# A ring of 32 message slots, with gathers written out, in a graph network kernel

## The reference

```python
xn = layernorm(x)
# graph part: one MLP for messages and nodes
mlp = lambda h: relu(h @ w1 + b1) @ w2 + b2
agg = segment_sum(mlp(xn[dst]), src, N)        # 50000 gathered rows, summed by src
gnn = mlp(xn + agg)
# mix part: 8 heads of 32, second-order linear attention over all nodes
q, k, v = split(xn @ Wqkv.T + bqkv)
y = 0.5*(qn x qn):(kn x kn x v) + c1*qn:(kn x v) + c2*sum(v)   # per head, divided by its first column
x = x + gnn + y @ Wproj.T + bproj
# FFN part: 16 experts, the top 2 of each node, 256 -> 512 -> 256
x = x + layernorm(xn2 + sum_k weight_k * expert_k(xn2)) * gamma + beta,  xn2 = layernorm(x)
```

## Time and profile before

| | us |
|---|---|
| median of 3 runs | 1543.14 (1540.83 to 1543.5) |
| the profiled execution | 1546.45 |
| its span, first to last instruction | 1544.5 |
| TensorE matmuls busy | 1125.4 (73%) |
| VectorE busy | 947.2 (61%) |
| GpSimd busy | 955.1 (62%) |
| ScalarE busy | 476.4 (31%) |
| mean granted TensorE clock | 0.855 of full |
| DMA, mean over the span | 94 GB/s |

### The profile page before, as it was taken

The page is one execution under the profiler, slowest core; times in us unless marked ns, Lnnn a source line. Parts: engine busy times, 40 slices in busy tenths (PEclk is TensorE's granted clock), DMA queues, the critical chain, the costliest instruction groups (busy, mean ns, idle before and its releaser), DMA issues.

```text
span 1544.5 us, 26303 instructions
## 1 busy us (share of the span) xinstructions
PE 1125.4 (73%) x7084; PEld 769.8 (50%) x7085; DVE 947.2 (61%) x2221; ACT 476.4 (31%) x1280; POOL 955.1 (62%) x1069
## 2 busy tenths in 40 slices
PE   2978878888846677667686767776884499999900
PEld 2656534333323444334453444444784499999800
DVE  4998989999955545445454555545356534433366
ACT  1555325555502223223222222221332032322302
POOL 4598339999976666666766667666000367755416
PEclk8999988999977878688877888878996699999955
DMA  5001000000034443444444455455462222222293
GB/s 154 26 26 34 21 21 1 0 0 0 0 102 119 130 131 117 128 132 122 129 124 129 127 153 156 128 155 123 128 219 93 81 69 70 73 70 70 61 236 100
DMA packets 57119, 145.11 MB, mean 94 GB/s; under 512 B 11117, under 2 KB 24909, under 8 KB 56944
## 3 DMA queue, kind: packets, MB, share of 16 engines
q0 software_dynamic: 33488, 101.80, 22.7%
q1 hardware_dynamic: 23584, 42.74, 9.4%
HBM read 124.91 MB, written 19.59 MB: 94 GB/s over the span
## 4 chain that ended last, share of the span: by engine, by line
PE 39%; DVE 18%; another core or an unknown queue 11%; POOL 11%; issue 10%; DMA 3%; DVEq 3%; ACT 2%; SPq 1%; POOLq 0%; ACTq 0%
PE bank L1805 8%; PE bank L2057 8%; PE bank L2068 7%; POOL big L698 6%; DVE node_buf L1269 3%; DVE big L1196 3%; POOL big L641 2%; DVE big L1195 2%; PE bank L1971 2%; PE bank L1858 2%; PE bank L1866 2%; DVEq L1269 2%; DMA x_buf<-x 1%; DMA big<-xn_rows 1%
## 5 line engine op out<-in xcount | busy, mean ns | idle before, releaser
L719 POOL DMA_INDIRECT big<-msg_rows,big x416 | 422.9, 1017 | 212.7 <-issue 102.0
L1269 DVE TENSOR_TENSOR node_buf<-node_buf,bank 125x256 f32 x416 | 174.6, 420 | 301.0 <-remote 131.1
L1805 PE MATMUL bank<-big 128*128 128x256 bf16 x1248 | 218.7, 324 | 63.1 <-DVE node_buf L1269 43.2
L1805 PEld LDWEIGHTS bank<-big 128*128 128x128 bf16 x1248 | 131.8, 114 | 141.3 <-DVE node_buf L1269 65.9
L1196 DVE TENSOR_SCALAR big<-bank,big 125x416 bf16<-125x416 f16 x400 | 184.6, 480 | 0.8 <-PE bank L1678 0.8
L954 ACT ACTIVATE big<-bank 128x500 f32<-128x500 f32 (+1 forms) x208 | 109.2, 572 | 222.8 <-remote 121.9
L698 POOL TENSOR_TENSOR big<-big 125x512 f32<-125x512 f32 x150 | 170.4, 1173 | 5.1 <-PE bank L1750 2.5
L1048 ACT ACTIVATE mid<-bank,const 128x128 f32<-128x128 f32 x256 | 73.0, 368 | 208.7 <-PE bank L2057 193.0
L1678 PE MATMUL bank<-big 125*128 125x416 bf16 x400 | 105.8, 350 | 29.9 <-DVE big L1196 19.6
L2068 PE MATMUL bank<-big,mid 128*128 x512 | 121.0, 380 | 0.0
L759 POOL DMA_INDIRECT moe_rows<-mid,const x64 | 71.7, 1120 | 78.7 <-DVE mid L1585 75.0
(11 more groups left out here) (307 smaller groups left out, 2119.2 us busy)
## 6 DMA issues: line engine op xcount, KB each, us to landing
big<-L_ffn_w SPq DMA_DIRECT2D x32, 512.0 KB
big<-msg_rows,big POOLq DMA_INDIRECT x416
big<-moe_rows SPq DMA_DIRECT2D x10, 560.0 KB
msg_rows<-big SPq DMA_DIRECT2D x25, 187.5 KB
xn_rows<-mid POOLq DMA_DIRECT2D x5, 625.0 KB, 5.8
x_buf<-x SPq DMA_DIRECT2D x5, 560.0 KB
big<-xn_rows SPq DMA_DIRECT2D x5, 560.0 KB
out<-big SPq DMA_DIRECT2D x5, 560.0 KB
```

The costliest lines, as they stand in the source:

```text
L719: pool.indirect_dma_start(msgs[k], None, msg_rows, bass.IndirectOffsetOnAxis(idx_ring[:, half, k:k + 1], 0)).then_inc(msgs_in[k], 16)
L1269: dve.tensor_tensor(rows, rows, agg_ps[2 * half + j][0:P, :], ALU.add).then_inc(s.agg_add, 1)
L1805: last = mm(agg_ps[k % 4], hot_src[:, turn, k, :], msgs[slot][:, D * i:D * i + D], start=i == 0, stop=i == 2, skip_group_check=True)
```

## The change

- The ring has 32 slots: the 25 node tiles' key and value columns, three at the end of `big`, and four in `mid`, two in the place of biases and two in that of the matrices `sel_f` and `selT`, which the key part's last transposes still use. Slots 2i and 2i + 1 share a semaphore; TensorE waits for 32 more on it before both messages.
- GpSimd's gathers are written out, 416 of them, with the index column read from `edge_idx` where it lies: no copy, no loop, no increment. Gather 16 waits for the last transposes of the key part (`kvT_mm`), gather n from 32 on for message n - 32 to be consumed.
- SP loads no expert during the message stage. All 16 are loaded after the last add, expert e after 3e // 2 additions of the second pass.

```diff
-        msgs = [big[:, 3 * D * k + D:3 * D * k + D + 3 * D // 2].bitcast(BF16) for k in range(2 * GB)]
+        slot_at = [big[:, 3 * D * k + D:3 * D * k + D + 3 * D // 2] for k in range(T)]
+        slot_at += [big[:, NX * 2048 - 3 * D // 2 * (k + 1):NX * 2048 - 3 * D // 2 * k] for k in range(3)]
+        slot_at += [mid[:, at_:at_ + 3 * D // 2] for at_ in (12 * D, 12 * D + 3 * D // 2, 4 * D, 4 * D + 3 * D // 2)]
+        msgs = [view.bitcast(BF16) for view in slot_at]
...
-            early = range(-(-2 * GB * 3 * D // 2048), phase // 2048)
-            for e in early:
-                sp.wait_ge(s.split_ok, (2048 * (e + 1) - 1) // (3 * D) + 1)
-                load_expert(e)
             sp.wait_ge(s.x_ok, CHUNKS)
             sp.dma_start(b1_rows, ffn_b1.rearrange("e (c p) -> (e c) p", p=128)).then_inc(s.b1_in, 16)
 
             sp.wait_ge(s.agg_add, NBATCH * GB)
-            for i, e in enumerate([e for e in range(NX) if e not in early]):
-                if i:
-                    sp.wait_ge(s.x2_add, 2 * i)
+            for e in range(NX):
+                if e:
+                    sp.wait_ge(s.x2_add, 3 * e // 2)
                 load_expert(e)
...
-            def gather(n, half):
-
-
-                pool.tensor_copy(idx_ring[:, half, :], edge_idx[:, bass.ds(n * 2 * GB, 2 * GB)]).then_inc(s.msg_idx_ok, 1)
-                pool.wait_ge(s.msg_idx_ok, n + 1)
-                for k in range(2 * GB):
-                    if not at(n, (0,)):
-                        pool.wait_ge(s.agg_mm, n * 2 * GB + k - (2 * GB - 1))
-                        apart(pool)
-                    pool.indirect_dma_start(msgs[k], None, msg_rows,
-                                            bass.IndirectOffsetOnAxis(idx_ring[:, half, k:k + 1], 0)).then_inc(msgs_in[k], 16)
-
-            gather(0, 0)
-            gather(1, 1)
-            with pool.Fori(1, NBATCH // 4) as i:
-                gather(i * 2, 0)
-                gather(i * 2 + 1, 1)
+            for n in range(NQ):
+                if n == 2 * GB:
+                    pool.wait_ge(s.kvT_mm, 4)
+                if n >= 4 * GB:
+                    pool.wait_ge(s.agg_mm, n - (4 * GB - 1))
+                slot = n % (4 * GB)
+                pool.indirect_dma_start(msgs[slot], None, msg_rows,
+                                        bass.IndirectOffsetOnAxis(edge_idx[:, n:n + 1], 0)).then_inc(msgs_in[slot // 2], 16)
...
-            def agg_pair(n, turn, q, rounds):
+            def agg_pair(n, turn, q, half, rounds):
...
+                first = (half * 2 + turn) * GB + 2 * q
+                pe.wait_ge(msgs_in[first // 2], rounds * 32)
                 for k in (2 * q, 2 * q + 1):
-                    slot = turn * GB + k
-                    pe.wait_ge(msgs_in[slot], rounds * 16)
+                    slot = first + k % 2
...
-                        agg_pair(half * 2 + 2 + k // 4, k // 4, k % 4, half + 2)
+                        agg_pair(half * 2 + 2 + k // 4, k // 4, k % 4, 1 - g, u + 1 + g)
```

More of the change, by code:

```diff
@@ L139, in __init__ @@
         self.sorted_ok = sem("sorted_ok")
-        self.msg_idx_ok = sem("msg_idx_ok")
         self.hot_src_ok = sem("hot_src_ok")
@@ L423, in program @@
         den_ones = b.take([CH], BF16, parts=1)
-        idx_ring = b.take([2, 2 * GB], I32)
         bucket_pack = b.take([NQ // 4], parts=1)
@@ L445, in program @@
         mixT = b.take([2, CH])
+        assert b.at + 9 * D // 2 <= NX * 2048
         kvT = big[:, features:features + 1024].rearrange("p (a n) -> p a n", a=2)
@@ L1925, in _ @@
             for q in range(4):
-                agg_pair(0, 0, q, 1)
+                agg_pair(0, 0, q, 0, 1)
             q_parts_T(0, 0, 2)
-            agg_pair(1, 1, 0, 1)
-            agg_pair(1, 1, 1, 1)
+            agg_pair(1, 1, 0, 0, 1)
+            agg_pair(1, 1, 1, 0, 1)
             gram_of(0, 0, 2)
-            agg_pair(1, 1, 2, 1)
+            agg_pair(1, 1, 2, 0, 1)
             den_of(0, 0, 2)
-            agg_pair(1, 1, 3, 1)
+            agg_pair(1, 1, 3, 0, 1)
             sel_of(0, 0, 0, 2)
```

## The result

The changed kernel takes 1532.81 us (median of 4 runs, 1531.99 to 1533.02); the kernel before, run beside it, takes 1543.27 us (1540.83 to 1543.5). The ratio is 0.9936, with a 95% interval of 0.992 to 0.9953: 10.5 us or 0.6% faster. The forecast was 1541.3 us, a gain of 1.8; the time lies inside the stated range, but the gain is almost six times the forecast one.

What follows compares the result with a forecast made beforehand. TensorE's message matmuls, losing up to 0.447 us per message while gathers are in flight, were taken to bound the message stage. 1543.14 less 1.8 (end -7.2, start +5.4, all else 0) gave 1541.3 us; range 1505 to 1557.

Steps and rivals of the forecast that it cites:

- "0 us; without that cover it would be -20.5" (copy, loop, increment): GpSimd's gathers: removing 0.79 us per turn of 16 gains 0, hidden behind 106 us of waiting for TensorE; otherwise -20.5.
- the large gain: Message stage: held results delay the next gather and twice the depth breaks this loop; 1532, 1500 or 1437 us; chance 0.14.
- the even part stays as it is: Message stage once the ring is full: each gather waits for one message consumed whatever the depth, 24.8 us per 16 messages.
- Tail, -7.2 us: End of the message stage: 32 messages instead of 16 remain after the last gather, saving 16 x 0.447 = 7.2 us.
- Filling, +5.4 us: Start of the message stage: 12 of 16 extra gathers fly beside TensorE's work, costing 12 x 0.447 = 5.4 us.
- The burst rival: Start of the message stage: a 20 us longer gather burst delays TensorE; +2, stronger case 1556, up to 1569; chance 0.26.
- The net of the ends, -1.8: Start and end of the message stage with 32 slots: -7.2 and +5.4 us together give -1.8 us.
- Pair semaphore, 0: TensorE's waits for messages: one semaphore for two slots removes 208 waits, priced at 0 us; 42.6 us at most.
- Expert loads, 0: Message stage: the three expert weight loads moved out of it aren't felt there, 0 us.
- Second pass, 0: After the last add: 20 MB move instead of 17, DMA doesn't set the pace; 0 us, up to 6 at the routing.
- The floor of 1.25 us for a gather: GpSimd in the message stage: a gather takes 0.95 us plus 0.30 of gap, also when written out.
- The signs: What traces would show: right, 24.8 us per 16 messages and GpSimd waits 100 or more; wrong, shrinking or filling over 10 longer.

Runs made afterwards that it cites:

- set one: Four kernels on one chip, kernel before 1474.35 us: 16 slots 0.9764, same with early expert loads 0.9772, only gathers written out 0.9872, only pair semaphore 0.9951.
- set three: One chip, kernel before 1552.87 us: 16 slots 0.9836, kernel before written out with copies 0.9872, 16 slots with third of bytes 0.9845, SyncE's loads instead of gathers 0.8517.
- set two: One chip, kernel before 1473.87 us: kernel before unedited 1.0002, the change 0.9762, 16 slots 0.9767, 32 slots opened slowly 0.9755.

## Why the prediction was right or wrong

- **"0 us; without that cover it would be -20.5" (copy, loop, increment): the step that failed.** Alone it gave 21.1 us in set one, where GpSimd sets the pace, and with only the copies kept 19.1 in set three, where GpSimd waits for held results; by the timelines the part taken away there is 15.9 us of GpSimd's time. The cover, 106 us of GpSimd's waiting for TensorE, wasn't one. Nor did it "only grow": it fell to 89.5. Of the step's 0.79 us per turn the copy is only 0.18, and the turn ahead of the loop shows that most of the rest isn't the loop. The rival of the large gain described such a loop, in which GpSimd's waiting is part of what delays it; it had 0.14. What shows is that GpSimd's own work lies on the path even there. By which route isn't settled. The end of the filling, where a result comes through as GpSimd has to stop, would fit a lock-step of the two: held results stop GpSimd, its stop lets them through, and GpSimd's own work and TensorE's waiting then add up instead of overlapping. No run tests this by itself.
- **"the even part stays as it is": wrong, by 21.1 us.** It measured 47.8 us for 32 messages after 49.8. Of the depth itself the step was nearly right: with 16 slots 16.6 of the 21.1 stay, and in set two depth changes nothing (0.9762 and 0.9767).
- **Tail, -7.2 us: right mechanism, half its size.** It measured -14.6. TensorE's idle time in the last 32 messages fell from 41.30 - 28.99 = 12.3 to 3.0 us, which is 9.3; the other 5.3 are busy time, 28.99 to 23.66, at a clock that rose from 0.83 to 1.00. The sum had priced idle time alone.
- **Filling, +5.4 us: wrong size, +22.7.** The reason given, "TensorE waits for another chain there", failed: the transposes of that chain ran 11 us earlier, and TensorE still stood for 25.07 us. The burst rival had this right. Its stronger case was 20 us lost, 7.2 won back, and with 16 slots in set three the filling is 65.9, as before.
- **The net of the ends, -1.8:** +22.7 - 14.6 = +8.1 by the windows. By these, 32 slots alone would have been a loss on this chip, less whatever of the even part's 21.1 is theirs (4.5 by the window with 16 slots).
- **Pair semaphore, 0: wrong where GpSimd sets the pace,** 7.0 us (4.3 to 10.2 by the interval); the 42.6 us of "issue" that I set aside as held results bounded it. Where results are held it wasn't tried alone.
- **Expert loads, 0: right.** 1439.10 and 1438.06 us. **Second pass, 0: right.** Outside the message stage the spans have 890.2 and 888.7 us (1.0 of the difference is the earlier first gather), and the distance at the routing stayed 6.9.
- **The floor of 1.25 us for a gather: right.** From one gather to the next it is 1.24 us at least and 1.25 in the median, in all 13 traces with gathers.
- **The signs.** Of those for being wrong, two came at once: the even part shrank (23.9 us per 16 messages where 24.8 were to stay), the sign of the large gain, and the filling grew by over 10 us, that of the burst. GpSimd's waits fell below the 100 us that the forecast wanted. Three pieces of 15 to 23 us made a net of 13, of which the forecast had 1.8. That the time fell inside the range was luck as much as anything: two rivals, one up and one down, came true together and cancelled for the most part.

## What to carry to other kernels

Waiting time on an engine is cover only if the engine isn't part of the loop that it waits on: here 106 us of waiting hid next to nothing of 20.5. Where a transfer or an issue slows its neighbours, price a deeper ring by its burst at the start, not only by its distance at the end; 16 slots lost nothing against 32 where nothing is held, and where results are held the filling cost 22.7 us against 14.6 won. The ring that opens slowly was no slower than either (0.9755) where it ran; whether it keeps the tail without the filling's loss where results are held wasn't run. 16 slots had 0.9836 on the third chip and the change 0.9936 in the first measurement, both with results held, so 16 slots look like the safer size of the two, though no one set compared them there.

## What the runs showed of the hardware

- With gathers issued by GpSimd, TensorE's results were held back on the chip of the first measurement and on that of set three, and on the two between not at all. For the kernel before, the message stage took 654.3 us on the first and 579.8 on that of set two; outside the stage the two spans agree (890.2 and 888.3). On the chip of set three the kernel before was timed (1552.87) but not traced. What differs between the chips is open.
- The hold doesn't go with bytes (131 and 44 GB/s: same) nor with DMA traffic as such (189 GB/s from SyncE: none). It goes with the gathers that GpSimd issues; whether with its work or with the scattered rows isn't separated.
- The two kinds of chip differ elsewhere too, which I can't explain: VectorE's 400 copies at L1196 (L1185), all done before the first gather, take 479 to 481 ns in the mean on the chips of the first measurement and of set three, and 529 to 578 on the two between. It is a mark of the chip and not of the hold: with SyncE's loads, where nothing is held, they take 479 as well.
- The granted clock went with the gaps: 0.80 to 0.84 in the even part with results held, 0.90 to 0.92 without, 0.99 with SyncE's loads. Of the 62.9 us between the even parts of the kernel before on the two kinds of chip (547.3 and 484.4), 29.2 are busy time of TensorE (391.65 and 362.46), at a clock of 0.80 and 0.92.
